# GpSimd adds two state-times-C products, and TensorE sums the added tile: one change to a four-stage kernel

## The reference, cut to what matters

```python
delta = softplus(dbc[..., :DT_RANK] @ dtw.T + dtb)
dA = jnp.exp(delta[..., None] * -jnp.exp(a_log))
mi = ALPHA * delta[..., None] * Bm[:, :, None, :] * xb[..., None]

def scan_fn(carry, inp):
    h, v = carry
    dA_t, mi_t, C_t = inp
    v = BETA * v + mi_t
    h = dA_t * h + v
    y_t = jnp.einsum('ben,bn->be', h, C_t)
    return ((h, v), y_t)
...
y = ys.transpose(1, 0, 2) + dp * xb
y = y * jax.nn.silu(z)
return jnp.einsum('ble,de->bld', y, ow)
```

## Time and profile before

| | us |
|---|---|
| median of three runs | 4493.16 |
| profiled execution | 4501.75 |
| its span, first to last instruction | 4500.1 |
| one stretch, most of the first Mamba layer | 1254 |
| TensorE busy over the span | 3545.9 |
| VectorE busy over the span | 2771.5 |
| GpSimd busy over the span | 2045.3 |

### The profile page before, as it was taken

How to read it: one execution, slowest core, us unless ns; L and a number is a source line. 1 busy time by engine, 2 the same in 40 slices (tenths; PEclk the granted TensorE clock), 3 DMA queues, 4 the chain that set the end, 5 groups by cost and what they waited for, 6 DMA issues and landing times. The chain is left out here.

```text
span 4500.1 us, 88368 instructions
## 1 busy us (share of the span) xinstructions
PE 3545.9 (79%) x28412; PEld 2364.2 (53%) x28413; DVE 2771.5 (62%) x4814; ACT 1979.1 (44%) x4446; POOL 2045.3 (45%) x1206
## 2 busy tenths in 40 slices
PE   6888869936889888898856988888888863199980
PEld 4554546614555555555534555555555533188870
DVE  3444432345877777777765777787777766255545
ACT  1212112216666565665625666566665632133320
POOL 0101000015666676666744666676666754500006
PEclk8888878968999999999978999999999985599995
DMA  1000000012222131221311213122131225411113
GB/s 49 0 0 0 0 21 0 0 55 59 56 57 69 48 74 51 58 69 50 75 35 47 66 50 76 48 66 59 51 76 50 70 71 187 143 47 47 47 38 109
DMA packets 152097, 244.92 MB, mean 54 GB/s; under 512 B 25714, under 2 KB 74130, under 8 KB 149012
## 3 DMA queue, kind: packets, MB, share of 16 engines
q1 hardware_dynamic: 142356, 212.69, 17.5%
q0 software_dynamic: 9344, 27.27, 1.8%
HBM read 119.89 MB, written 38.27 MB: 35 GB/s over the span
## 5 line engine op out<-in xcount | busy, mean ns | idle before, releaser
L893 POOL TENSOR_TENSOR m_hc<-m_h,m_Cb 128x1024 f32<-128x1024 f32 x512 | 1205.0, 2354 | 769.3 <-DVE m_h L1014 443.9
L1014 DVE TENSOR_TENSOR_SCAN m_h<-m_dA,m_hlast,m_bank 128x256 f32<-128x256 f32 x2048 | 1354.4, 725 | 144.6 <-PE m_bank L1295 66.3
L1277 PE MATMUL m_bank<-m_hc,ident 128*128 128x512 f32 x2048 | 1209.6, 680 | 146.7 <-POOL m_hc L893 146.3
L1144 ACT ACTIVATE m_dA<-m_delta,m_rate 128x256 f32<-128x256 f32 x2048 | 894.2, 500 | 16.1 <-DVE m_h L1014 15.1
L1293 PEld LDWEIGHTS m_bank<-m_M,m_U 128*128 128x128 bf16 x8192 | 606.6, 101 | 362.5 <-DVE m_h L1014 221.4
L1293 PE MATMUL m_bank<-m_M,m_U 128*128 128x64 bf16 x8192 | 676.8, 197 | 127.4 <-DVE m_h L1014 112.6
L1295 PEld LDWEIGHTS m_bank<-m_M,m_U 112*128 112x128 bf16 x8192 | 580.2, 101 | 205.1 <-issue 173.2
L1295 PE MATMUL m_bank<-m_M,m_U 112*128 112x64 bf16 x8192 | 677.1, 197 | 0.0
L1277 PEld LDWEIGHTS m_bank<-m_hc,ident 128*128 128x128 f32 x2048 | 338.0, 204 | 195.7 <-POOL m_hc L893 163.2
L962 DVE SCALAR_TENSOR_TENSOR m_cv<-m_xpre,m_conv,m_cv 128x256 f32<-128x256 f32 x384 | 272.7, 752 | 22.5 <-ACT m_cv L1082 18.0
L1207 PE MATMUL m_bank<-m_pair,m_in 128*128 128x256 f32 x1024 | 269.4, 390 | 7.5 <-ACT m_cv L1082 3.8
(11 more groups left out here) (260 smaller groups left out, 5580.6 us busy)
## 6 DMA issues: line engine op xcount, KB each, us to landing
m_Cb<-m_c_rows SPq DMA_DIRECT2D x256, 256.0 KB, 3.2
m_M<-m_Mhi SPq DMA_DIRECT2D x128, 256.0 KB, 4.1
m_M<-m_Mlo SPq DMA_DIRECT2D x64, 256.0 KB, 3.9
m_U<-m_Uhi SPq DMA_DIRECT2D x128, 128.0 KB, 3.2
slots_x<-x_res SPq DMA_DIRECT2D x40, 256.0 KB, 4.1
x_x_in<-slots_x SPq DMA_DIRECT2D x40, 256.0 KB, 2.6
slots_y<-x_y POOLq DMA_DIRECT2D x40, 256.0 KB, 2.3
m_U<-m_Ulo SPq DMA_DIRECT2D x64, 128.0 KB, 3.4
```

The costliest lines, as they stand in the source:

```text
L893: nc.gpsimd.tensor_tensor(hc[:, n % 2], h[:, n % RING], Cb[:, g % 2, n % NG, :].unsqueeze(1).broadcast_to([P, KI, CM]), ALU.mult).then_inc ...
L1014: nc.vector.tensor_tensor_scan(h[:, n % RING, m, :], dA[:, n % RING, m, :], VB[(n % 2) * 2 + g][:, (m % 2) * CM:(m % 2 + 1) * CM], hlast[: ...
L1144: nc.scalar.activation(dA[:, n % RING, m, :], delta[:, par, m, :], ACT.Exp, scale=rate[:, m, n:n + 1]).then_inc(s["da_done"], 1)
L1277: last = nc.tensor.matmul(Y[half][:], net.ident[:], hc[:, n % 2, 2 * half:2 * half + 2, :], start=(n == 0), stop=(n == NS - 1))
```

## The change

For the pairs of steps 0 and 1, 2 and 3, 10 and 11, 12 and 13 of each block, GpSimd adds the two products into the second tile after the second product. TensorE leaves out the accumulation of the first step of the pair, and the accumulation of the second takes the sum. `TWO` holds the second steps. A new counter `two_done` counts the adds. The accumulation of a second step waits for it in place of `hc_done` and counts `acc_done` up by two. The product behind a pair waits for the add in place of an accumulation. The first accumulation of a block is now that of step 1. The other eight steps (4 to 9, 14 and 15) are as before.

```diff
+        TWO = (1, 3, 11, 13)
+        twos = lambda n: sum(1 for m in TWO if m <= n)
...
                     pool.wait_ge(s["scan_done"], 1 + AHEAD + (k + 1) * KI + next_scan)
-                    pool.wait_ge(s["acc_done"], 1 + AHEAD + k - 1)
+                    if n - 1 in TWO:
+                        pool.wait_ge(s["two_done"], 1 + c * len(TWO) + twos(n - 1))
+                    else:
+                        pool.wait_ge(s["acc_done"], 1 + AHEAD + k - 1)
...
+                    if n in TWO:
+                        pool.wait_ge(s["hc_done"], 1 + AHEAD + k + 1)
+                        pool.sem_inc(net.carrier, 1)
+                        nc.gpsimd.tensor_tensor(hc[:, 1], hc[:, 0], hc[:, 1], ALU.add).then_inc(s["two_done"], 1)
...
                 def accumulate(c, n, half):
                     k = c * NS + n
-                    if half == 0:
+                    if n + 1 in TWO:
+                        return
+                    if half == 0 and n in TWO:
+                        pe.wait_ge(s["two_done"], 1 + c * len(TWO) + twos(n))
+                    elif half == 0:
                         pe.wait_ge(s["hc_done"], 1 + AHEAD + k + 1)
-                    if n == 0:
+                    if n == 1:
                         pe.wait_ge(s["gate_done"], 1 + c * KI + 2 * half + 2)
                     last = nc.tensor.matmul(Y[half][:], net.ident[:], hc[:, n % 2, 2 * half:2 * half + 2, :],
-                                            start=(n == 0), stop=(n == NS - 1))
+                                            start=(n == 1), stop=(n == NS - 1))
                     if half == 1:
-                        last.then_inc(s["acc_done"], 1)
+                        last.then_inc(s["acc_done"], 2 if n in TWO else 1)
```

More of the change, by code:

```diff
@@ L706, in mamba_phase @@
                  "mf_done mhi_done mlo_done halo_done carry_psum chi_done clo_done moved_next moved "
-                 "v_psum da_done scan_done hlast_done hc_done acc_done y_psum gated_done out_psum xm_done rate_done "
+                 "v_psum da_done scan_done hlast_done hc_done two_done acc_done y_psum gated_done out_psum xm_done rate_done "
                  "floor_done const_done c_kept c_spread0 c_spread1").split()
```

## The result

| | before | after |
|---|---|---|
| median, us | 4493.31 | 4655.35 |
| runs, us | 4486.39 to 4494.0 | 4643.34 to 4659.64 |
| ratio, with its 95% interval | | 1.0353 [1.0339, 1.0367] |
| profiled span, us | 4500.1 | 4650.2 |
| mean granted clock of TensorE | 0.866 | 0.844 |

(The kernel before has four runs here; the part ahead of the prediction has three of them.) The change makes the kernel 162 us slower. The forecast was 4538, with a range up to 4595: the sign was right, the size was not. An inner block now lasts 84.74 us where it lasted 79.86 (means over 24 blocks, 12 in each layer), so 4.9 us per block are to be explained where 1.13 were forecast. Of all executions reported here one is counted as slow, 9537 us for pair_2_3_reordered, and it is left out of that kernel's median and ratio.

A forecast was written before the change was run, and what follows sets the result against it. It took GpSimd then TensorE as the path in steps 1 to 5, the softplus chain in 6 to 10, TensorE in 11 to 15. +1.13 us per block times 30 (+34), +3 and +8 gave +45: 4538 us, range 4465 to 4595.

The forecast's parts named there:

- The add: GpSimd's add taken as 2.35 us; with hand-overs the sum is ready 4.85 us after the second product's start, instead of 2.41.
- Steps 1 to 5: From product 1 to the delta matmuls the path is GpSimd, then TensorE in program order, with no slack before accumulation 1.
- +0.58 us: Cost per block at the delta matmuls: accumulation 1 starts 2.44 us later, less 1.86 given back by removing accumulation 2.
- Rival C: Before accumulation 1, the old clock dip passes while TensorE stands still: -53 and +11, 4451 us; chance 0.13, half version 0.08.
- Steps 6 to 10: The path passes through VectorE's and ScalarE's softplus chain; no pair of the change is there, and no cost was counted.
- Steps 11 to 15: TensorE is the bound, GpSimd a short distance ahead; +0.47 us for pair 10 and 11, +0.08 for 12 and 13.
- The whole 1.86 us saved turns into waiting: At pair 10 and 11, TensorE reaches accumulation 11 2.52 us after product 11 and waits until 4.85: +0.47 us.
- TensorE's clock: I put the net effect at 0: Longer idle before accumulation 1 and new waits of about 2.3 and 1.9 us later were given no net clock cost.
- Rival B: Waits before accumulations 11 and 13 pull the clock down, 1.7 us per dip, one per block: +54, 4592 us; chance 0.18.
- Its sign: Sign for Rival B: a granted clock in the layers lower than 0.93 by 0.02 or more.
- TensorE is the bound: In steps 11 to 15 TensorE works without a gap, busy 12.00 of 12 us, and sets the pace.
- rival D: TensorE bounds everywhere and the adds hide behind its work: 7.4 us saved per block, 238 in 32, 4255 us; chance 0.02.

The follow-up runs named there:

- pair_2_3_reordered: Changed kernel with only pair 2 and 3 added, and GpSimd's second `matrix` and first `matrix_low` each behind a later product: 4436.42 us, ratio 0.986 to the kernel before.
- only_0_1: Changed kernel with only the pair of steps 0 and 1 added on GpSimd: 4587.99 us against 4497.48 for the kernel before, ratio 1.0202.
- late_gpsimd: Kernel before with three small memsets on GpSimd behind product 4 of each block, no pair added: 4522.92 us, ratio 1.0059, +24.7 us.
- only_10_11: Changed kernel with only the pair of steps 10 and 11 added on GpSimd: 4559.48 us against 4497.48 for the kernel before, ratio 1.0135.
- only_10_11_filled: Only pair 10 and 11 added, with zero matmuls of the same size on TensorE replacing accumulation 10: 4521.9 us, ratio 1.0053 to the kernel before.
- filled: Changed kernel with all four adds, and zero matmuls of the same size on TensorE replacing accumulations 10 and 12: 4597.73 us, ratio 1.0236 to the kernel before.
- no_add: Changed kernel without the four adds and their waits, so y lacks states 0, 2, 10 and 12: 4476.19 us, ratio 0.9963 to the kernel before.

## Why the prediction was wrong

**The add: right.** 2.35 us were taken, 2347 ns is the mean. The hand-over to itself was taken as 0.09 from L851 to L853, and is 0.18 in each pair shown. The distance is 4.93 to 5.01 in place of 4.85. That is 0.1 to 0.2 us per pair, and with it GpSimd's path was forecast well.

**Steps 1 to 5: the right path, a low price.** Accumulation 0 freed nothing, accumulation 2 gave its 1.86 back. The step "+0.58 us" is 1.29 at the delta matmuls: the distance is 5.01 instead of 4.85, and the clock's dip, which the kernel had before as well, is longer. In the record of the clock it lasts 10.2 us in each of the 24 inner blocks, where it lasted 3.4 in 14 and 6.8 in 10. Rival C, that the longer idle time would let the dip pass, is refuted: the dip moves and grows with the idle time. Of the 0.7 us 0.16 are the distance. The other half a microsecond also stands in only_0_1, which takes nothing from TensorE behind the pair: its delta matmuls come 3.05 us later, where the distance grew by 2.60. That it is the dip's is likely, and no run tried it.

**Steps 6 to 10: "no pair of the change is there".** This step failed. No add stands there, but GpSimd's whole chain comes about 2.2 us later, and VectorE's two softplus pieces, which had met the last 0.3 and 1.0 us of its products, now meet the last 1.2 and 1.9 (their means less 1.09). That is +0.93 us per block (2.22 less 1.29). late_gpsimd brought such a loss about alone, 24.7/32 = 0.77, and in pair_2_3_reordered it is gone. The prediction asked of the later GpSimd only who waits for it by a semaphore. This wait is none, so no view of waits has it; it shows as a longer duration of another engine's instruction. The trace of before had the sign of it: L979, with the same operation and size as L974, took 2060 ns against 1394.

**Steps 11 to 15: "The whole 1.86 us saved turns into waiting" is right, "TensorE's clock: I put the net effect at 0" is the step that failed.** This is the largest part, 2.7 us per block where 0.55 were forecast. The accumulations start 4.93 us after their second products, but behind the new wait before accumulation 11 the clock falls. The wait is longer than forecast too, 3.78 us in the block shown against 2.3: only_10_11, where GpSimd is not late, has the forecast 2.28, and here GpSimd comes 2.0 us late to product 11 and TensorE, freed of accumulation 2, by less. Behind the second new wait, before accumulation 13, the clock fell in only 5 of the 24 inner blocks. only_10_11_filled shows the size for one pair, 38 us or 1.2 per block; filled shows 58 us or 1.8 for both. Rival B had this mechanism and this place, with 1.7 us per dip, at a chance of 0.18. Two things spoke for more: the two dips of a block both followed short idle times, and the section of the Trainium skill that the prediction names says what idle gaps do. Against them stood one wait of 2.18 us at clock 1.00, and it was held to speak for all of them. The trace of before has this wait, before accumulation 7, in 30 blocks (1.98 to 2.31 us), and in 11 of them the clock behind it is 0.65 to 0.73. One of the 11, first and second half of accumulation 7:

```profile
1341.97 1.12 PE L1277 MATMUL m_bank<-m_hc,ident 128*128 128x512 f32 x2 [2.18 <-POOL m_hc L893]
...
1343.45 2.06 PE L1277 MATMUL m_bank<-m_hc,ident 128*128 128x512 f32 x2
```

So the rows of before, read over all blocks, gave rival B more than its 0.18. Its sign came as well: the clock in the layer is 0.88, lower than 0.93 by more than 0.02. B's own time, 4592, was still 63 too low, since nothing in it paid for steps 6 to 10, for the longer early dip or for the longer wait before accumulation 11.

**"TensorE is the bound" in steps 11 to 15** held only for a little: rival D's 238 us were not there to be had. no_add, with no adds to wait for, gets 22 of them.

The account per block, from the runs of single pairs: forecast +2.44 - 1.86 + 0.47 + 0.08 = +1.13; measured +2.83 - 1.05 + 1.94 + 0.57 = +4.29, and 5.06 with all four together. The 0.77 between are not settled; half a microsecond of it may lie between the two late pairs, within what the runs leave uncertain.

## What to carry to other kernels

When an engine's work is added or moved, look at what every other engine does at the new time, not only at who waits for it: a VectorE instruction with two SBUF inputs waited out the GpSimd instruction under way (a mean of 1.39 us became 2.30, one of 2.06 became 2.97), and in the profile that is only a duration that differs between equal instructions. Work saved on TensorE that turns into a wait may cost more than the work did, since the clock falls behind the wait; so put such a saving where no wait comes of it (pair 2 and 3 here), and price a new wait of 2 us with a dip until a trace shows otherwise, read over all blocks and not in one. Try the parts of a change one by one: here one of four was a gain, and with two GpSimd instructions moved it was worth 1.4%.

## What was unexpected in the hardware

- The turn-taking goes both ways, one instruction at a time. While VectorE's piece takes its 1.09 us, the next GpSimd instruction stands: `matrix_low` behind product 6 takes 3.12 us before the change and 3.11 after, where the shortest of its 64 is 2.12. The product under way when the piece comes keeps its 2.36.
- A wait of 2.28 us inside a stretch at full clock was enough for a mean clock of 0.68 in the 3.50 us behind it, and in another place a wait of 2.18 us left it at 1.00, as such waits did in 19 of 30 blocks of the kernel before, and not in the other 11. What decides between the two, no run here shows.
- An instruction of GpSimd that waits for its own engine's last one starts 0.18 us after its end, in 122 of the 128 adds of the changed kernel (0.49 at most).
